# Cross-attention: the mask of 8 score tiles in 12 is added by VectorE instead of by a TensorE matmul

## The reference

```python
x = x + attn(layernorm(x))              # delta rule on blocks of 4 x 512 tokens, then an MLP
x = x + xattn(layernorm(x), ctx, mask)  # cross-attention, the stage that the change touches
x = x + ffn(layernorm(x))               # 6 routed experts and a shared one

def xattn(query, key, mask):            # 16 heads of 16 channels
    Q, K, V = split(query @ wq.T), split(key @ wk.T), split(key @ wv.T)
    scores = einsum('bhqd,bhkd->bhqk', Q, K) / sqrt(16)
    scores = where(mask[:, None] == 1, -1e9, scores)     # mask: (32, 112, 375) int32
    return merge(softmax(scores) @ V) @ w_out.T
```

## Time and profile before

| | |
|---|---|
| median of 3 runs | 1670.47 us (1670.46 to 1671.88) |
| profiled execution | 1662.81 us, span 1661.0 us |
| mean granted TensorE clock | 0.981 |
| PE busy | 1558.4 us (94%) |
| PEld busy | 1351.4 us (81%) |
| DVE busy | 973.8 us (59%) |
| ACT busy | 680.5 us (41%) |
| POOL busy | 289.6 us (17%) |
| chain that ended last | PE 71%, DMA 7%, SP's queue 7%, DVE 4% |
| L811, mask matmuls | 384, 143.2 us busy |
| L1545, maxima | 512, 261.0 us busy, 179.0 us idle before them |

### The profile page before, as it was taken

How to read it: one execution, slowest core, us unless ns; L and a number is a source line. 1 busy time by engine, 2 the same in 40 slices (tenths; PEclk the granted TensorE clock), 3 DMA queues, 4 the chain that set the end, 5 groups by cost and what they waited for, 6 DMA issues and landing times.

```text
span 1661.0 us, 35301 instructions
## 1 busy us (share of the span) xinstructions
PE 1558.4 (94%) x12448; PEld 1351.4 (81%) x12448; DVE 973.8 (59%) x2720; ACT 680.5 (41%) x1430; POOL 289.6 (17%) x269
## 2 busy tenths in 40 slices
PE   5899999998886999999999999999989999999998
PEld 5898889987774777777777777777789999999998
DVE  5657655675543555555555555555475566556655
ACT  3443434343323444445454554444633323332332
POOL 2323322233322111111111111110330000000000
PEclk9999999999987999999999999999999999999999
DMA  7100000000127777777777777775210000000000
GB/s 171 33 1 0 0 0 0 0 0 18 26 47 116 109 109 108 104 105 105 104 105 104 104 104 104 104 106 69 58 52 12 11 0 11 11 11 0 11 11 12
DMA packets 85736, 89.58 MB, mean 54 GB/s; under 512 B 45056, under 2 KB 73216, under 8 KB 85680
## 3 DMA queue, kind: packets, MB, share of 16 engines
q1 hardware_dynamic: 84944, 88.52, 33.4%
q0 software_dynamic: 160, 0.23, 0.1%
q10 hardware_dynamic: 576, 0.07, 0.0%
HBM read 36.92 MB, written 3.67 MB: 24 GB/s over the span
## 4 chain that ended last, share of the span: by engine, by line
PE 71%; DMA 7%; SPq 7%; DVE 4%; issue 3%; ACT 2%; POOL 1%; DVEq 0%; ACTq 0%; POOLq 0%
PE psum L920 17%; PE psum L560 15%; PE psum L939 9%; SPq L355 7%; DMA qst<-negm 7%; PE psum L796 5%; PE psum L831 5%; PE psum L811 3%; PE psum L817 3%; PE psum L768 2%; PE psum L681 2%; PE psum L667 2%; PE psum L678 2%; PE psum L549 1%; PE psum L844 1%
## 5 line engine op out<-in xcount | busy, mean ns | idle before, releaser
L1545 DVE CUSTOM_DVE_ANT_0 junk<-psum,biasq 112x375 f32<-112x375 f32 x512 | 261.0, 546 | 179.0 <-PE psum L796 147.3
L1191 ACT ACTIVATE pr<-psum 125x448 f32<-125x448 f32 x384 | 206.1, 546 | 193.6 <-PE psum L817 189.2
L817 PE MATMUL psum<-qst,kst 97*125 97x224 f32 x768 | 247.4, 351 | 0.0
L796 PE MATMUL psum<-kst,qst 96*112 96x376 f32 x512 | 169.7, 354 | 9.9 <-DMA qst<-qlo 7.0
L1298 ACT ACTIVATE sg<-psum 128x448 f32<-128x448 f32 x112 | 60.9, 545 | 249.5 <-PE psum L920 247.5
L811 PE MATMUL psum<-flagk,negbig 125*125 125x448 bf16 x384 | 143.2, 373 | 18.7 <-DMA qst<-negm 18.7
L831 PE MATMUL psum<-pr,vaug 125*32 125x112 f32 x3072 | 153.2, 271 | 1.0 <-ACT pv L1196 0.9
L817 PEld LDWEIGHTS psum<-qst,kst 97*125 97x125 f32 x768 | 145.6, 190 | 5.1
L920 PE MATMUL psum<-h3hi,ehi 128*128 128x448 f32 x448 | 135.2, 381 | 0.0
L920 PE MATMUL psum<-h3hi,elo 128*128 128x448 f32 x448 | 133.8, 377 | 0.0
L920 PE MATMUL psum<-h3lo,ehi 128*128 128x448 f32 x448 | 133.8, 378 | 0.0
(11 more groups left out here) (243 smaller groups left out, 3319.0 us busy)
## 6 DMA issues: line engine op xcount, KB each, us to landing
kst<-khi SPq DMA_DIRECT2D x64, 376.0 KB, 6.9
kst<-klo SPq DMA_DIRECT2D x32, 376.0 KB, 10.1
ctxT<-in_ctxT SPq DMA_DIRECT2D x32, 375.0 KB, 4.4
qst<-qhi SPq DMA_DIRECT2D x128, 56.0 KB, 5.4
stage<-in_e SPq DMA_DIRECT2D x21, 256.0 KB, 2.9
maskq<-in_mask SPq DMA_DIRECT2D x32, 164.1 KB
maskk<-in_maskT SPq DMA_DIRECT2D x32, 164.1 KB
x_res<-in_x SPq DMA_DIRECT2D x8, 448.0 KB, 11.9
```

The costliest lines, as they stand in the source:

```text
L796: pe.matmul(bank[max_bank(n, hd)][0:T, 0:S2E], head(qst[par][0:ROWS], hd), pair(kst[par][0:ROWS], hd // 2), start=True, stop=True).then_in ...
L817: mm = pe.matmul(bank[q % 3][0:KP, cols(i, 2 * T)], pair(kst[par], n)[:, cols(q // HPB, KP)], both, start=False, stop=True, skip_group_che ...
L1191: nc.scalar.activation(pr[q % PROBS][:].rearrange("k i q -> k (i q)"), bank[q % 3][0:KP, 0:GT], ACT.Exp, scale=1.0 / HD ** 0.5).then_inc(s ...
L1545: nc.vector.tensor_tensor_reduce(out=junk[:, hd % 2, :], in0=bank[max_bank(n, hd)][0:T, 0:S2], in1=biasq[:, par, :], scale=1.0, scalar=-3e ...
```

## The change

In slots 1, 3, 5, 7, 8, 9, 10 and 11 of each row (`BY_DVE`) the mask matmul is left out, and the first `score` matmul opens the bank. VectorE adds biask (0 or -2^40 by key and query, float32) to the scores as it reads them out of PSUM, into one of two SBUF tiles `ms`, and ScalarE's exponential reads that tile. Slots 0, 2, 4 and 6 stay as they are. GpSimd makes biask beside biasq and flagk. The new tiles lie in what was a gap in SBUF. A bank is free for TensorE when VectorE's addition (`masked`) has read it, in the slots of `BY_DVE`, and the exponential in the others. In slots 0 to 7 the addition stands between the two maxima of its slot; `normalise` and `low_context` stay behind the loop over q.

```diff
+BY_DVE = (1, 3, 5, 7, 8, 9, 10, 11)
+DVE_SLOTS = len(BY_DVE)
...
+        def done_by_dve(b, q):
+
+            return DVE_SLOTS * (b + q // SLOTS) + sum(x <= q % SLOTS for x in BY_DVE)
...
                 nc.gpsimd.tensor_scalar(biasq[:, par, :], maskq[:], 1.0, -BIG, ALU.is_equal, ALU.mult)
+                nc.gpsimd.tensor_scalar(biask[:, par], maskk[:], 1.0, -BIG, ALU.is_equal, ALU.mult)
                 nc.gpsimd.tensor_scalar(flagk[:, par], maskk[:], 1.0, None, ALU.is_equal).then_inc(s2["flags"], 1)
...
-                pe.wait_ge(s2["exp"], SLOTS * b + q + 1)
+                before = (q - 3) % SLOTS
+                if before not in BY_DVE:
+                    pe.wait_ge(s2["exp"], SLOTS * b + q + 1)
+                elif q >= 3 or not is_row(b, 0):
+                    pe.wait_ge(s2["masked"], done_by_dve(b, q - 3))
+                if q in BY_DVE:
+                    return
                 flags = flagk[:, par, q // HPB, :].unsqueeze(1).broadcast_to([KP, HPB, T])
...
-                mm = pe.matmul(bank[q % 3][0:KP, cols(i, 2 * T)], pair(kst[par], n)[:, cols(q // HPB, KP)], both, start=False, stop=True, skip_group_check=True)
+                mm = pe.matmul(bank[q % 3][0:KP, cols(i, 2 * T)], pair(kst[par], n)[:, cols(q // HPB, KP)], both, start=q in BY_DVE, stop=True, skip_group_check=True)
...
-                act.wait_ge(s2["sc_ps"], done + 1)
+                if q in BY_DVE:
+                    scores = ms[BY_DVE.index(q) % 2][:].rearrange("k i q -> k (i q)")
+                    act.wait_ge(s2["masked"], done_by_dve(t * RB + par, q))
+                else:
+                    scores = bank[q % 3][0:KP, 0:GT]
+                    act.wait_ge(s2["sc_ps"], done + 1)
...
+            def bias_scores(t, par, q):
+                b = t * RB + par
+                nth = BY_DVE.index(q)
+                dve.wait_ge(s2["sc_ps"], SLOTS * b + q + 1)
+                if nth >= 2:
+                    dve.wait_ge(s2["exp"], SLOTS * b + BY_DVE[nth - 2] + 4)
+                elif not is_row(b, 0):
+                    dve.wait_ge(s2["exp"], SLOTS * (b - 1) + BY_DVE[nth - 2] + 4)
+                bias = biask[:, par, q // HPB, :].unsqueeze(1).broadcast_to([KP, HPB, T])
+                nc.vector.tensor_tensor(ms[nth % 2][:], bank[q % 3][0:KP, 0:GT].rearrange("k (i q) -> k i q", i=HPB), bias, op=ALU.add).then_inc(s2["masked"], 1)
...
                 for q in range(SLOTS):
                     if following >= 1 and q < HEADS // 2:
-                        maxima(*nxt, (2 * q, 2 * q + 1))
+                        maxima(*nxt, (2 * q,))
+                    if q in BY_DVE:
+                        bias_scores(t, par, q)
+                    if following >= 1 and q < HEADS // 2:
+                        maxima(*nxt, (2 * q + 1,))
```

More of the change, by code:

```diff
@@ L189, in decoder_layer @@
                 kst[i] = w2(f"kst{i}", [ROWS + 1, PPC, DC, S2E], F32R)
-                w2(f"gap_k{i}", [P, PPC, DC, S2E])
+                if i == 0:
+                    biask = w2("biask", [KP, RB, KC, T])
+                    ms = [w2(f"ms{n}", [KP, HPB, T]) for n in range(2)]
+                    w2("gap_k0", [P, PPC * DC * S2E - RB * KC * T - 2 * HPB * T])
+                else:
+                    w2(f"gap_k{i}", [P, PPC, DC, S2E])
                 vaug[i] = w2(f"vaug{i}", [KP, KC, HEADS, 2 * HD])
@@ L226, in decoder_layer @@
         s = {n: sem(n) for n in names + [f"stage{i}" for i in range(STAGES)]}
-        s2 = {n: sem("c_" + n) for n in """cleared ctx_in c_hi c_lo mask_in ready bn flags stat rs h hT_ps hT_sb q_ps q_hi q_lo k_ps k_hi k_lo v01_ps v_ps v_sb qst0 qst1 qst2 kst0 kst1 kst2
+        s2 = {n: sem("c_" + n) for n in """cleared ctx_in c_hi c_lo mask_in ready bn flags masked stat rs h hT_ps hT_sb q_ps q_hi q_lo k_ps k_hi k_lo v01_ps v_ps v_sb qst0 qst1 qst2 kst0 kst1 kst2
             max_ps smax mt_ps negm negm_in sc_ps exp pv_done pv_sb ot_ps rden on onT_ps onT_sb wo_ps x_new""".split()}
@@ L1188, in exponentials @@
                 done = SLOTS * (t * RB + par) + q
-                act.wait_ge(s2["sc_ps"], done + 1)
+                if q in BY_DVE:
+                    scores = ms[BY_DVE.index(q) % 2][:].rearrange("k i q -> k (i q)")
+                    act.wait_ge(s2["masked"], done_by_dve(t * RB + par, q))
+                else:
+                    scores = bank[q % 3][0:KP, 0:GT]
+                    act.wait_ge(s2["sc_ps"], done + 1)
                 act.wait_ge(s2["pv_done"], done + 1)
-                nc.scalar.activation(pr[q % PROBS][:].rearrange("k i q -> k (i q)"), bank[q % 3][0:KP, 0:GT], ACT.Exp, scale=1.0 / HD ** 0.5).then_inc(s2["exp"], 1)
+                nc.scalar.activation(pr[q % PROBS][:].rearrange("k i q -> k (i q)"), scores, ACT.Exp, scale=1.0 / HD ** 0.5).then_inc(s2["exp"], 1)
             def copy_pv(t, par):
```

## The result

| | before | after |
|---|---|---|
| median of the runs | 1670.47 us | 1787.26 us (4 runs, 1784.96 to 1795.77) |
| ratio to the runs of before | | 1.073, 95% interval 1.070 to 1.075 |
| profiled execution, span | 1662.81, 1661.0 us | 1786.06, 1783.9 us |
| mean granted clock | 0.981 | 0.937 |
| 700 to 1100 us: TensorE busy, granted clock | 390.0 us, 1.00 | 348.2 us, 0.91 |

A forecast was written before the change was run, and what follows sets the result against it. Transfers from kst to negm bound the kernel before; after, VectorE's loop would, at 23.1 us a row. 52 us over 28 rows, +1 at the end, +8 for the clock: +61, so 1730 us, range 1698 to 1768.

The forecast's parts named there:

- What bounds the kernel: Before the change: the transfers from kst's issue to slot 0, negm landing last, 14.5 us; not TensorE.
- The loop of VectorE: Slot 9 to next first maximum 5.6 us, from there to slot 9 17.5: 23.1 a row against 21.26, +1.85.
- The step of 0.54 us an addition: VectorE's additions out of PSUM, eight a row: 0.54 us from start to start, bounds 0.47 and 0.62.
- the longer h: End of normalise: h takes 0.74 us instead of 0.41, as GpSimd's mask work starts in the same moment.
- the walk through slots 1 to 7: row_max waits for VectorE's maxima give back 0.19, 0.33, 0.11 and 0.62 us in slots 1, 4, 5 and 6.
- low_context's place: On VectorE behind the last additions and normalise: starts 4.7 us after slot 9's start, next first maximum at 5.6.
- The exponential out of SBUF: Eight ScalarE exponentials reading SBUF, not PSUM: no added time, bounds -0.05 and +0.05 us each.
- Rival B: low_context held by GpSimd: +0.7 us a row if by biasq alone (1750), 3.15 if by the batch (1818); 13%.
- The clock: TensorE's clock falls where idle time meets a row's start: 0.3 us a row, bounds 0 and 1.7; +8 us.
- rival C: TensorE's clock falls in every row: 1.4 us a row more than taken, 1770 us; 12%.
- The cost of GpSimd's pass: GpSimd's added mask pass takes 1.4 us; kst may move 0.3 us late, under cover of 1.1 left.
- The ends: At the end, normalise_group's work against mask matmuls saved in rows 29 to 31: -3 to +4 us, taken +1.

The follow-up runs named there:

- Run 8: Kernel before, without the change: context loaded ahead of the masks, k projection, its copies and so kst one slot earlier; 1645.68 us, ratio 0.987.
- run 2: Changed kernel plus nine matmuls of unused result a row on TensorE, three ahead of slot 0 and six in slot 1; 1756.30 us, ratio 1.054.
- run 4: Changed kernel with VectorE's additions in slots 1, 3, 5 and 7 only; 1687.75 us, ratio 1.014.
- run 3: Changed kernel with VectorE's loop over the rounds written out, same instructions and order; 1769.06 us, ratio 1.061.
- Run 6: Kernel before plus GpSimd's pass for biask alone, read by nobody; 1694.83 us, ratio 1.017.
- run 9: Run 8's kernel plus additions in slots 8 and 10, biask for a third of the keys, normalise back behind slot 7; 1659.11 us, ratio 0.996.
- 5: Changed kernel with VectorE's additions in slots 8, 9, 10 and 11 only; 1743.23 us, ratio 1.044.
- 10: Run 8's kernel plus additions in slots 2, 3, 8 and 10, GpSimd's full pass, normalise back behind slot 7; 1677.58 us, ratio 1.006.
- run 1: Changed kernel with normalise back behind slot 7, ahead of the additions of slots 8 to 11; 1767.79 us, ratio 1.056.
- 11: Run 8's kernel plus the change as it was made, all eight additions; 1771.09 us, ratio 1.062.
- run 7: Changed kernel with normalise back behind slot 7, three and two filler matmuls on TensorE, VectorE's loop written out; 1707.04 us, ratio 1.023.

## Why the prediction was wrong in size and right in kind

- **What bounds the kernel: right.** Run 8 shows it by moving kst earlier.
- **The loop of VectorE: right.** Forecast 5.6 + 17.5 = 23.1 us; measured 5.49 + 17.5 in run 2's undisturbed rows. The step of 0.54 us an addition, the longer h (0.58 us; 0.74 forecast), the walk through slots 1 to 7 (17.6 in run 4, 17.69 by the walk) and low_context's place hold. The exponential out of SBUF takes 0.03 us more than the one out of PSUM before (576 and 546 ns), inside its bounds, though not for the reason given: two durations always lie on one line. Against 21.33 us it is 1.7 us a row, 47 of the 123 us between the profiled executions.
- **Rival B: not in this kernel.** After the change biasq starts 0.56 us ahead of low_context in every row, and neither is longer for it (1.50 and 0.93 us):

```profile
846.56 1.50 POOL L502 TENSOR_SCALAR biasq<-maskq 112x375 f32<-112x375 int32 x1
```

The row at 471.99 had said so the earlier trace rows. By the rule of the Trainium skill (SBUF — State Buffer, "Who interferes with whom") low_context would have waited for the end of biasq. At other distances between the two there is a wait, and the last section says how far the rule holds.
- **The clock: the step that failed.** "Bounds 0 and 1.7 a row; I take 0.3, some rows having it." Measured: about 1.7 a row (25.20, less 23.0, less 7 x 1.95 / 28 = 0.5 for the loop's end), some 48 us where the sum had 8. Every row has a piece of low clock, so the term was at its bound and not near nothing. The argument against rival C, "slot 0's work breaks the gap", looked at the two gaps by themselves. Measured, slot 0 has 1.6 us of work between a gap of 0.64 and one of 1.59, and over 846.64 to 850.04 TensorE was busy 1.81 of 3.40 us, much as it was ahead of the low clock of the earlier trace rows. The prediction had even more idle time there, "two gaps of more than 1 us, before and after slot 0", so its own numbers spoke for rival C in every row. Run 2 shows the clock's part by filling the gaps. The prediction's own sign for C, a stage clock under 0.95, came true at 0.91.
- **The loop's end on VectorE: not in the forecast.** 1.95 us in seven rows, 14 us by the rows and 18 by run 3's median. Run 3 shows it. In the kernel before it was 0.29 us, ahead of a maximum that waited for TensorE anyway.
- **The cost of GpSimd's pass: sized wrongly.** "kst may move 0.3 us late, under cover of the 1.1 left." Run 6 gives 27 us in the kernel before. In the changed kernel VectorE's loop is later than the transfers, so it should cost less; what it takes there wasn't measured. Every mended version has it too, and none was run without it.
- **The ends:** forecast +1, measured 5.5 ahead of row 1 and 9 behind row 28. Their causes were not followed up.

47 + 48 + 14 + 14 = 123 us, the difference of the profiled executions (1786.06 - 1662.81), where the prediction had 52 + 8 + 0 + 1 = 61. On the medians it is 117, because the median of before lies 7.7 us above its profiled execution and that of after 1.2; the prediction had carried the 7.7 over.

## What to carry to other kernels

When work moves to an engine that is in order, what counts isn't its busy share but what comes to stand behind the new instructions: here normalise, low_context and the next row's maxima, and with slot 8, an exponential and negm. Once the new loop leaves TensorE idle in pieces, price its clock from a stretch of the trace in which TensorE sat idle in the same way, and put that price in full into each row in which the pieces recur. And a few tenths of a us of cover on a chain of transfers is none: a pass of 1.3 us ahead of the loads cost 27 us. Work that comes with a change on another engine is worth a run by itself.

## What was not expected of the hardware

**The end of VectorE's loop.** In the kernel before the next instruction of VectorE's program comes 0.29 us after the loop's branch at 835.28, and after the change 2.86 us (819.28 to 822.14), where the loop turns; VectorE's own idle time is the 1.88 us shown above, since h and low_context still run at first. All seven turns have it, 2.75 to 3.02 us. The other engines' loops take 0.16 to 0.3 us in both. The Trainium skill (Runtime: NRT & Kernel Launch, "Instruction fetch mechanics") says that a taken branch whose target isn't in the window already fetched forces a fetch. That the loop had grown past such a window fits, and the runs bear it out, though none was made for it. From branch to branch the trace has this many records of VectorE, waits and branches included:

| records a turn | kernels | from the branch to the next instruction, us |
|---|---|---|
| 253 | before, runs 6 and 8 | 0.29 |
| 271 | run 9 (slots 8, 10) | 0.29 |
| 286 to 289 | runs 4, 5 and 10 (four additions) | 0.29 |
| 319 | after, runs 1, 2 and 11 (eight additions) | 2.75 to 3.07 |

The order of the work differs among the runs of 319 and the gap doesn't. So it goes with the length and comes between 289 and 319 records. No run lengthened the loop by anything but additions and their waits, so that it is the length itself stays an argument. TensorE's turn has some 1280 records and no such gap.

**VectorE and GpSimd.** low_context (two SBUF inputs) and GpSimd's biasq meet in every kernel, at different distances:

| first | by, us | low_context, us | biasq, us | |
|---|---|---|---|---|
| low_context | 0.44 | 0.94 | 1.86 | before |
| low_context | 0.00 | 0.94 | 2.31 | run 7 |
| biasq | 0.01 | 1.30 | 1.50 | run 7 |
| biasq | 0.07 | 1.23 | 1.50 | run 1 |
| biasq | 0.56 | 0.93 | 1.50 | after |

When VectorE is first, biasq takes longer by 0.36 us or by 0.81, some 0.13 us less than what is left of low_context. When biasq is first, low_context takes 0.36 us longer if it starts at once, 0.2 if it starts 0.16 us later (a row of run 1), and at most 0.02 from 0.34 us on, but for one row of run 9 (1.18 us in all). So the second is held, as the rule of the Trainium skill named with rival B says, but VectorE only at the start of GpSimd's instruction and not for the whole of it. The 1.86 us for biasq in the earlier trace rows, one of the two bounds for the new pass, had such a wait in it; the pass itself was sized well (1.4 us, measured 1.34).

**The clock.** Its cost didn't follow the change's own time. Run 1 made VectorE's loop 1 us shorter and had more of the low clock (19 pieces of 6.8 us, three of 10.2, one of 17.1; mean 0.925). With five matmuls of filler a row and the loop written out, run 7 had three pieces of 3.4 and one of 13.7 (mean 0.969) and was 61 us faster.
